# Rows kept in a region of DRAM for each expert, the experts moved to between superblocks 4 and 5, and part of the weight splitting moved to GpSimd

## The reference

```python
xn = (x - mean) / sqrt(var + 1e-5)
# branch 1, per batch of 2048 tokens
s = xn @ W_spin.T + b_spin
scores = (s @ W_J.T) @ s.T / sqrt(128);  local = softmax(scores) @ s
a = tanh(beta * (s + mean(s) @ W_global.T + local))
# branch 2, per token
logits = xn @ Wg.T + bg
top2 of logits -> experts e1, e2, weights softmax(top2)
gu = xn @ Wgu[e] + bgu[e];  gate = min(gu[::2], 7);  up = clip(gu[1::2], -7, 7)
y_e = ((up + 1) * gate * sigmoid(1.702 * gate)) @ Wd[e] + bd[e]
out = x + a + w1 * y_e1 + w2 * y_e2
```

## Time and profile before

| | us |
|---|---|
| median of 3 runs | 362.35 |
| lowest, highest | 361.89, 365.35 |
| the profiled execution | 362.15 |
| its span | 360.4 |
| busy: TensorE, VectorE | 324.9 (90%), 309.9 (86%) |
| busy: ScalarE, GpSimd | 256.8 (71%), 203.7 (57%) |
| attention, steps 0 to 71 | 36.2 to 173.9 |
| scatters of GpSimd (line 517) | 87.2 to 172.7 |
| expert groups, line 536 of GpSimd | 187.8 to 255.4 |
| gathers of GpSimd (line 547) | 266.0 to 349.7 |
| last exponent (step 127) | 346.1 |

### The profile page before, as it was taken

The page is one execution under the profiler, slowest core; times in us unless marked ns, Lnnn a source line. Parts: engine busy times, 40 slices in busy tenths (PEclk is TensorE's granted clock), DMA queues, the critical chain, the costliest instruction groups (busy, mean ns, idle before and its releaser), DMA issues.

```text
span 360.4 us, 5972 instructions
## 1 busy us (share of the span) xinstructions
PE 324.9 (90%) x1778; PEld 271.9 (75%) x1779; DVE 309.9 (86%) x630; ACT 256.8 (71%) x509; POOL 203.7 (57%) x271
## 2 busy tenths in 40 slices
PE   1878999998999999999978999999899998989980
PEld 1666788776777778888768999999788786867750
DVE  5988979999978999999769999888878999987855
ACT  2754777876699797687646988888787586578751
POOL 4276851325777777777113444534137777777760
PEclk9978999999999999999999999999999999999996
DMA  5999710000111211212222877765543354555551
GB/s 148 325 332 340 282 35 0 1 31 7 51 51 54 80 46 53 90 51 82 74 87 75 241 222 229 235 207 178 178 117 107 104 164 123 131 145 133 133 126 34
DMA packets 41359, 45.97 MB, mean 128 GB/s; under 512 B 3770, under 2 KB 33082, under 8 KB 41330
## 3 DMA queue, kind: packets, MB, share of 16 engines
q1 hardware_dynamic: 36162, 32.94, 29.1%
q0 software_dynamic: 5168, 12.67, 12.4%
HBM read 23.46 MB, written 22.12 MB: 126 GB/s over the span
## 4 chain that ended last, share of the span: by engine, by line
PE 40%; DVE 22%; POOL 19%; issue 8%; ACT 5%; DMA 4%; POOLq 0%; SPq 0%; ACTq 0%; DVEq 0%
POOL made L547 9%; POOL gy L547 8%; PE PS L556 8%; PE PS L558 8%; PE PS L557 8%; DVE mx L1121 6%; DVE pl L1106 5%; PE PS L609 4%; PE PS L661 2%; PE PS L786 2%; PE PS L771 2%; DVE stats L1077 2%; DMA xy<-slots_x 1%; PE PS L788 1%; PE PS L791 1%
## 5 line engine op out<-in xcount | busy, mean ns | idle before, releaser
L921 ACT ACTIVATE PS<-PS 128x512 f32<-128x512 f32 x128 | 74.8, 585 | 42.8 <-PE PS L558 41.2
L1106 DVE TENSOR_TENSOR pl<-PS,ph 128x512 fp32r<-128x512 f32 x128 | 87.7, 685 | 14.1 <-ACT ph L932 13.5
L1121 DVE TENSOR_REDUCE mx<-PS 128x1 f32<-128x512 f32 x128 | 84.3, 682 | 6.0 <-PE PS L609 6.0
L932 ACT ACTIVATE ph<-PS 128x512 fp32r<-128x512 f32 x128 | 76.5, 598 | 12.1 <-PE PS L558 0.8
L517 POOL DMA_INDIRECT slots_x<-xn,posu x64 | 63.0, 985 | 19.7 <-issue 17.1
L609 PE MATMUL PS<-xT,gq 128*128 128x512 f32 x128 | 49.5, 423 | 6.6 <-DVE mx L1121 6.3
L556 PE MATMUL PS<-gq,xT 128*128 128x512 f32 x128 | 52.4, 410 | 1.5 <-ACT gq L937 0.8
L556 PE MATMUL PS<-ph,rows 128*128 128x512 f32 x128 | 51.5, 402 | 1.8 <-DVE pl L1106 1.8
L558 PE MATMUL PS<-gq,xT 128*128 128x512 f32 x128 | 50.1, 391 | 0.0
L558 PE MATMUL PS<-ph,rows 128*128 128x512 f32 x128 | 50.1, 391 | 0.0
L557 PE MATMUL PS<-pl,rows 128*128 128x512 f32 x128 | 50.0, 391 | 0.0
(11 more groups left out here) (199 smaller groups left out, 682.8 us busy)
## 6 DMA issues: line engine op xcount, KB each, us to landing
slots_y<-yr SPq DMA_DIRECT2D x20, 512.0 KB, 3.1
slots_x<-xs SPq DMA_DIRECT2D x1, 5120.0 KB, 22.0
xy<-slots_x SPq DMA_DIRECT2D x20, 256.0 KB, 3.0
xn<-in_L_attn_x SPq DMA_DIRECT2D x8, 256.0 KB, 5.5
w_f<-in_L_ffn_Wgu SPq DMA_DIRECT2D x1, 2048.0 KB, 12.8
late<-in_L_ffn_Wgu SPq DMA_DIRECT2D x1, 2048.0 KB, 18.3
xs<-in_L_attn_x SPq DMA_DIRECT2D x8, 256.0 KB, 3.5
out_y<-made SPq DMA_DIRECT2D x7, 256.0 KB, 3.3
```

Source lines behind the costliest of these rows:

```text
L921: A(S[:, n % 3], S[:, n % 3], ACT.Exp).then_inc(exp_done, 1)
L932: A(ph[:, i % RING], S[:, n % 3], ACT.Copy).then_inc(s_hi, 1)
L1106: v.tensor_tensor(dst, S[:, n % 3], high.bitcast(F32), ALU.subtract).then_inc(s_lo, 1)
L1121: v.tensor_reduce(mx4[:, a, c:c + 1], MX[:, n % 2], AX.X, ALU.max).then_inc(mx_free, 1)
```

## The change

- **Regions.** `slots_x` and `slots_y` have 33 tiles for each expert (and 16 tiles of zeros behind them), so a row's place no longer depends on other experts' counts. The places of batch 0 are known once batch 0 is counted: the first scatters are issued from step 16 of VectorE on, those of batch 1 follow. The scatters go batch by batch, in eights.
- **A list of tiles.** VectorE makes a list of 80 tiles (first those that batch 0 alone fills, then the rest), with the expert and the row number of each. A group's four tiles don't lie side by side any more: SyncE loads four row numbers into registers and issues four DMAs for the rows, and again for the results. Instead of the 5 MB of zeros, one DMA clears 16 tiles and 16 DMAs write zeros behind the last row of each expert.
- **The row** has 129 columns, the weight last, so the rewriting of column 0 and its wait go.
- **MOE_AT is 64**, the boundary between superblocks; `oT_part` goes.
- **Low parts** of the weights of experts 8 to 15 are made by GpSimd among its scatters.
- **After the experts**, `add_parts` is on GpSimd between its gathers, and a superblock is combined every 7 steps.

```diff
-    MOE_AT = 5 * TB - 4
+    MOE_AT = 4 * TB
+    ETILES = NT + 1
+    REGION = ETILES * P
+    ROWS = (NE * ETILES + NE) * P
...
-        COUNT_AT = {16: 0, 17: 1}
+        COUNT_AT = {13: 0, 19: 1}
...
-        WEIGHT_LO_AT = {**{28 + n: (n,) for n in range(4)}, **{40 + n: (n,) for n in range(4, 8)},
-                        **{60 + n: (8 + 2 * n, 9 + 2 * n) for n in range(4)}}
+        WEIGHT_LO_AT = {30: (0,), 31: (1,), 37: (2,), 41: (3,), **{40 + n: (n,) for n in range(4, 8)}}
...
+                def rows_at(which):
+                    _, rows = nc.values_load_multi_w_load_instructions(
+                        which, engines=(mybir.EngineType.SP,), min_val=0, max_val=ROWS - P,
...
+                    return rows
...
+                def group_in(g):
+                    for a, row in enumerate(rows_at(tile_of[:, 1, 4 * g:4 * g + 4])):
+                        sp.dma_start(xy[:, g % 2, a], slots_x[bass.ds(row, P)]).then_inc(xg_in[g % 2], 16)
+
+                def rows_in(g):
                     sp.wait_ge(t_fill, rows_fill(g) + 1)
-                    sp.dma_start(xy[:, u], slots_x_v[:, bass.ds(4 * g + 8, 4)]).then_inc(xg_in[u], 16)
+                    sp.wait_ge(w_kept, g + 1)
+                    group_in(g + 2)
...
-                    sp.dma_start(slots_y_v[:, bass.ds(4 * g - 8, 4)], yr[:, u]).then_inc(y_out[u], 16)
+                    for a, row in enumerate(rows):
+                        sp.dma_start(slots_y[bass.ds(row, P)], yr[:, u, a].bitcast(U32)).then_inc(y_out[u], 16)
...
+                for g in range(2, NG + 2):
+                    if g + 2 <= NG - 3:
+                        rows_in(g + 2)
...
+                    results_out(g)
                     if g < NG:
                         bias_in(g, g % 2)
...
+            def ranks_of(b):
+                pool.wait_ge(e_free, e_no["R", b] + 1)
+                g.tensor_tensor(KEY[:, of(b)], OH1[:, of(b)], RANK[:, of(b)], ALU.mult).then_inc(route_pool, 1)
+                g.tensor_tensor(PROD[:, of(b)], OH2[:, of(b)], RANK[:, of(b)], ALU.mult).then_inc(route_pool, 1)
...
+                    for q in range(2):
+                        n = 4 * b + 2 * c + q
+
+                        if c:
+                            pool.wait_ge(scat[b][q], 128)
+                        part = slice(b * TB + 8 * q, b * TB + 8 * q + 8)
+                        g.tensor_copy(xn[:, part, D], w12[:, c, part]).then_inc(weights_in, 1)
+                        pool.wait_ge(weights_in, n + 1)
+                        for t in range(part.start, part.stop):
+                            pool.indirect_dma_start(slots_x, ...)
+                        if n == 0:
+                            list_consts()
+                            share_one(1)
+                            share_two(1)
+                        if n == 1:
+                            ranks_of(1)
...
+                        if n in (4, 5):
+                            for k in range(NE // 2 + 4 * (n - 4), NE // 2 + 4 * (n - 3)):
+                                pool.wait_ge(w_hi, k + 1)
+                                g.tensor_tensor(wl[:, k], w_f[:, k], wh[:, k].bitcast(F32), ALU.subtract).then_inc(w_lo, 1)
...
+            def places(b):
+                for c in range(2):
+                    dve.wait_ge(route_pool, 4 * b + 3 + c + 2 * (1 - b))
+                    v.tensor_reduce(mk[:, 6, b * TB:b * TB + TB], (KEY, PROD)[c][:, b * TB:b * TB + TB], AX.X, ALU.add).then_inc(dchain, 1)
...
+                    v.tensor_copy(posu[:, c, b * TB:b * TB + TB], mk[:, 6, b * TB:b * TB + TB]).then_inc(routed, 1)
...
+            SHARE_AT = {13: 0, 22: 1}
+            RANKS_AT = {15: 0, 21: 1}
+            PLACES_AT = {16: 0, 23: 1}
+            LIST_AT = {25: 0, 26: 1, 28: 2, 29: 3}
...
-            BOTH_AT = {MOE_AT + 11 + 6 * k: k for k in range(7)}
-            PARTS_AT = {MOE_AT + 12 + 6 * k: k for k in range(7)}
-            FINISH_AT = {MOE_AT + 13 + 6 * k + 2 * (k == 6): k for k in range(7)}
+            BOTH_AT = {MOE_AT + 11 + 7 * k: k for k in range(7)}
+            FINISH_AT = {MOE_AT + 18 + 7 * k: k for k in range(6)}
+            FINISH_AT[126] = 6
```

More of the change, by code:

```diff
@@ L68, in sem @@
             return ctx.enter_context(nc.semaphore(name))
[L70 to L75, removed]
+        xn = sb("xn", [P, NT, D + 1])
+        (made,), (gu_sb,), (xT0,) = over((("made", [P, 4, 4, 2 * D], F32),), (("gu_sb", [P, 2, 2, 512], F32),),
+                                         (("xT0", [P, 2, N], F32R),))
         xT = [xT0, sb("xT1", [P, 2, N], F32R)]
@@ L136, in build, with small @@
         wgu0 = late[:].rearrange("p (e n) -> p e n", e=NE)
[L137 to L142, removed]
+        bufs = [late[:, 512 * k:512 * k + 512] for k in range(5)]
+        KEY, OH1, OH2, RANK, PROD = (w.rearrange("p (t e) -> p t e", t=NT) for w in bufs)
+        scans = [late[:, 2560 + 272 * k:2560 + 272 * k + 272] for k in range(4)]
+        MASK, DATA, EX0, EX1 = (w.rearrange("p (e t) -> p e t", e=NE) for w in scans)
+        cut = [3648]
+        def small(n):
+            cut[0] += n
+            return late[:, cut[0] - n:cut[0]]
+        rev, first_row, first_row_up = small(NE), small(NE), small(NE)
+        tiles_v, ones_v = small(NV), small(NV)
+        before_v, at_v, step_v, start_v, expert_v, reached, steps_on = (small(NV + 1) for _ in range(7))
+        tile_at, expert_at = small(1), small(1)
         def slot_hl(k):
@@ L318, in _ @@
                 tokens_in(1)
+                sp.wait_ge(pads_ready, 1)
+                for n in range(0, NE, 4):
+                    for row in rows_at(pad_i[0:1, n:n + 4]):
+                        sp.dma_start(slots_x[bass.ds(row, P)], zer[:]).then_inc(pads, 16)
                 sp.wait_ge(eid_ready, 1)
@@ L328, in bias_in @@
                 def bias_in(g, u):
[L329 removed]
+                    if g >= 2:
                         sp.wait_ge(y_done, 2 * g - 2)
[L331 removed]
+                    sp.dma_start(wb[0:2, u].bitcast(F32), b_slots[:, 512 * g:512 * g + 512]).then_inc(b_in[u], 16)
                 sp.wait_ge(b_kept, 16)
@@ L702, in count_pairs @@
                 o = e_bank("R", k)
-                pe.wait_ge(oh_ready, 2)
-                mm(o, (onesb, tri)[k][:], ohb, start=True, stop=True).then_inc(e_fill, 1)
+                pe.wait_ge(oh_ready, k + 1)
+                for n in range(2):
+                    m = mm(o[:, n * TB * NE:(n + 1) * TB * NE], (onesb, tri)[n][:], ohb[:, k * TB * NE:(k + 1) * TB * NE],
+                           start=True, stop=True)
+                m.then_inc(e_fill, 1)
             def fields(k, h):
@@ L973, in step @@
                     spins_out(*use)
-                if j == 2 and k:
+                if j == 2 and k and k != MOE_AT // TB:
                     values_hi(k - 1)
```

406 lines of the change are left out of this document (206 added, 200 removed).

## The result

The changed kernel takes 406.38 us (median of 4 runs, 406.23 to 408.72), the kernel before 363.55 us beside it: ratio 1.119, 95% interval 1.112 to 1.127. The forecast was 379 us, with a range up to 397. The sign is right; the size falls short by 27 us. The profiled execution took 406.23 us, its span is 404.5.

What follows compares the result with a forecast made beforehand. TensorE (90% busy) and VectorE (86%) were taken as full in turn, the expert stage as TensorE's. 362.15 - 4.6 - 4 - 1.3 - 2 + 10 + 2 + 2 + 15 = 379 us, range 359 to 397.

Steps and rivals of the forecast that it cites:

- Item 9: Expert stage: SyncE's nine DMAs and two register loads take 4.8 us a group against 3.47; +15 us, bounds 4 to 35.
- Item 5: Step 23: VectorE stands for batch 1's ranks, queued on GpSimd behind two eights of scatters; +10 us (8 to 12).
- Item 7: Behind the stop at step 23: TensorE's granted clock near half after idling slows its products; +2 us (0 to 4).
- Item 6: Steps 13 to 29: VectorE's extra list instructions, half-size reductions and a wait for GpSimd's share; +2 us (1 to 3).
- Items 2: Combining, steps 88 to 111: additions move to GpSimd, the rest falls every 7 steps; three stretches about 14 us each, -4 us.
- item 3: Steps 56 to 63: eight low parts leave VectorE, so the stretch falls from 14.76 to 13.40 us; -1.3 us.
- Item 4: Turned rows: TensorE's 4.0 us wait for maxima goes, with the rewritten column's wait; -2 us.
- Item 1: Kernel's end: gathers finish some 20 us before the last step, so VectorE's 4.62 us wait goes; -4.6 us.
- Item 8: GpSimd's last scatter at about 172 us, hidden before step 64 at 173; without Item 5's stop, some 5 us wait.
- B: Rival, expert stage: SyncE keeps pace with small DMAs under 0.30 us, adding nothing; 364 us, chance 0.14.
- C: Rival, step 23: earlier scatters hold nobody up, so the kernel gets faster; 352 us, or 357; chance 0.16.
- D: Rival: zero-writing DMAs delay the list of tiles, or unaligned rows double the scatters' cost; over 400 us, chance 0.04.

Runs made afterwards that it cites:

- e4: Changed kernel with one DMA for a group's four rows and one for its four results, at fixed places; 415.08 us on a chip with pauses.
- h3: Changed kernel with one DMA for a group's rows and one for its results, at fixed places; 375.30 us, ratio 1.035 to the kernel before.
- e3: Changed kernel with only a group's four results put into one DMA, at a fixed place; 432.60 us on a chip with pauses.
- f2: Changed kernel with batch 1's ranks behind the first eight scatters and list constants made before all scatters; 399.61 us, ratio 1.101 to the kernel before.
- h2: Changed kernel with early ranks in their old place, low parts on VectorE, one DMA each for a group's rows and results; 362.31 us, ratio 0.9998.
- f1: The changed kernel itself, run again on another chip; 410.07 us, ratio 1.123 to the kernel before.
- e1: Same edit as f2 to the changed kernel, on a chip with pauses; 452.89 us beside 470.76 of the kernel before.
- f4: Kernel before with low parts of experts 8 to 15 on GpSimd behind its last scatter; 363.14 us against 362.91, ratio 1.0014.
- h1: Kernel before with the last superblock's VectorE additions reordered, gathered halves added one by one; 362.16 us against 362.19, ratio 0.9982.
- g1: Same edit as h1 to the kernel before, on a chip with pauses; ratio 0.9954.

## Why the prediction was wrong, by its steps

**Item 9 is the step that failed, in its size.** The mechanism was as forecast: SyncE back to back, TensorE waiting for rows. I took 0.46 us for a DMA of a tile, the spacing of DMAs with a fixed address at the kernel's start, and counted 0.04 of arithmetic inside it. Measured are 0.53: with an address in a register there are two register instructions and five gaps of 0.03 to 0.06 around each issue. A round was forecast at 4.8; it takes 5.47 without a wait and 5.68 on the average. Groups then were 5.70 us apart, 2.23 above TensorE's pace, over thirteen gaps: 29 us in place of 14 x 1.3 less 3. The 3 us that the doubled buffers should lend were not seen. e4 and h3 give 29 us back, so +15 should have been +29. This alone is 14 of the 27 us: 7 for the 0.07 us too little on each of eight DMAs, 5 for the rest of the round and its waits, 2 for the lent time less one round that was not slow. The row with 0.59 in the loop, which I kept as an upper bound, was the nearest in kind (same loop, arithmetic included); I went by shape instead. The Trainium skill's "Runtime: NRT & Kernel Launch", section Instruction fetch mechanics, would have given 28 us for this item; its sum came out near, but not by its reason: the load of four registers took 0.36 us here (the median of 40), 0.09 a register. In e3, where a round has one load only, the same load took 1.01, for which I have no reason.

**Item 5: right,** 10.29 us of stop (forecast 10). **Item 7: wrong in its price.** The granted clock behind the stop was 0.50, as forecast, but f2 leaves 0.3 us for it and not 2, because VectorE went on setting the pace. The rest is the 1.41 us wait at 90.53, which the forecast had nowhere. That 12 in all was forecast and f2 gives 12.1 is luck.

**Item 6: right** (+2.4: start of step 0 to step 32 of h2 against before, 69.22 to 66.78). What I did not forecast is the start: step 0 begins at 38.16 us instead of 36.16. It varies between executions of one kernel (38.16 and, in f1, 35.95; with one edit 36.81 in e1 and 39.29 in f2), so it may be chance.

**Items 2, 3, 4: no gain, 7.3 us forecast.** f4 shows it for item 3. The row for steps 56 to 63 in the earlier trace rows had TensorE busy 14.76 of 14.76 us, so VectorE's low parts could not have been what set it; I took the shortest stretch, 13.40 us, as the floor of all stretches, though its TensorE has 60 products and the other 72. Item 2 fails in the same way: steps 88 to 111 fall from 46.1 to 43.9 us, but 80 to 87 and 112 to 119, the light ones before, rise by 1.0 and 1.4 (the additions now fall there too), and steps 80 to 119 together are 70.9 and 71.1. In the changed kernel's window of steps 72 to 79 TensorE is the full one:

```profile
298.35:312.93 14.58, 14.42 (x69) 11.73 (x68) 11.79 (x24) 11.01 (x20) 11.51 (x12) 1.00 0.36 102
```

Item 4: the wait did go. TensorE's products and weight loads at the turned rows stood 4.1 and 5.5 us in all before and 0.2 and 0.9 in h2. But steps 56 to 79 with the experts take 118.82 us in both: behind the experts h2 needs 17.33 us for steps 64 to 71, where 13.40 were enough before. What makes this stretch longer was not looked into.

**Item 1: right in its size, not in its reason**, -4.45 for -4.6. h1 takes the wait alone away and gains nothing, so the wait was not what the late gathers cost. The last gather now comes 12.4 us ahead of the last exponent (forecast some 20), early enough for whatever follows it.

**Item 8 and the scatters: hidden, but later than forecast.** The first scatter came at 78.7 (forecast 74), of which 2 are the later start, the last at 180.4 (172), for GpSimd waited for high parts too. Without the stop the cover is gone, as the item says: f2 loses 3.5 us there. What was not in the list at all is that GpSimd's chain held VectorE: +2.6 us in the changed kernel, +5 in f2.

Misses: 14 (item 9) + 7.3 (2, 3, 4) + 2.6 (held VectorE) + 2 (start) + 0.8 (the rest) = 27. **Rivals:** B fell with the 3.46 of h3 against 5.7: SyncE doesn't keep pace. C fell with the stop at step 23. D had over 400 us, but its reasons fell: the scatters are 1.26 us apart as before, and the first group starts 6.0 us behind step 63 in the changed kernel as in h2, which loses nothing. The range failed since it was drawn from a sum whose largest term stood in the lower third of its bounds of 4 to 35, and the gains were given no chance of being nothing.

## What to carry to other kernels

A loop that a slow queue feeds is priced by the period of one round in the same kind of loop, register instructions and gaps included, and compared with the time of the engine it feeds; 0.07 us a DMA was 7 us here. A gain may be taken off a stretch only if the row of the stretch shows the relieved engine full and the others not. And work may be taken to GpSimd only after looking at what waits behind it there.

## What the runs showed of the hardware

- A VectorE `tensor_tensor` with both operands in SBUF (0.67 us) stood while GpSimd ran `tensor_tensor`s back to back: 1.23 us beside one (e1), 3.05 beside three, 4.79 beside four. It ended 0.55 or 0.56 us behind GpSimd's last one each time. The operands decide: beside GpSimd's second chain of four in f2 (150.88 to 154.82) VectorE's reductions from PSUM took their usual 0.68 us and its `tensor_tensor`s with one operand in PSUM their 0.69, and the one with both in SBUF that began at 154.46 ended 0.56 behind the chain.
- Behind the 11.25 us in which TensorE stood, it was granted half its clock (0.50), and its products came 0.43 us apart instead of 0.23. The steps lost 0.3 us at most by it, since VectorE was the full engine.
- Issues of DMAs by SyncE with a register address: 0.53 us from one to the next, whether 64.5 or 128 KB. Rows of 516 bytes landed after 2.0 us for 64.5 KB, and h3's groups kept TensorE's pace with them.
- Some 4 us at the end of h1 in which the profile shows nothing, 10.8 us behind the last gather; with that gather 26 us ahead of the end (g1) they are not there. The cause is open.
- On three chips all kernels had unexplained pauses, and the kernel before (470 us) was slower there than the changed kernel without its stop (453 us). A verdict from such a chip would have had the wrong sign.
